# Layer 2's linear attention and graph convolution change places in a four-layer graph transformer kernel

## The reference, cut to what matters

```python
xn = _layernorm(x)
x = x + _L2_gnn_ref(xn, edge_index, W, b) + _L2_mix_ref(xn[None], Wq, bq, Wk, bk, Wv, bv, Wo, bo)[0]
x = x + _L2_ffn_ref(_layernorm(x)[None], ...)[0]

# _L2_gnn_ref: graph convolution, loops added to the edges
norm = deg_inv_sqrt[src] * deg_inv_sqrt[dst]
out = segment_sum((x @ W)[src] * norm[:, None], dst) + b

# _L2_mix_ref: linear attention, 12 heads of 64
q, k, v = elu1(x @ Wq + bq), elu1(x @ Wk + bk), x @ Wv + bv     # elu1(t) = elu(t) + 1
kv, ksum = einsum('bhnd,bhne->bhde', k, v), k.sum(axis=2)
out = (einsum('bhld,bhde->bhle', q, kv) / einsum('bhld,bhd->bhl', q, ksum)) @ Wo + bo
```

## Time and profile before

| what | value |
|---|---|
| median of 3 runs | 3227.3 us (3222.09 to 3234.06) |
| profiled execution, time | 3223.88 us |
| profiled execution, span on the core | 3222.1 us |
| PE busy | 3017.0 us (94%), mean granted clock 0.97 |
| PEld, DVE, ACT, POOL busy | 2340.4, 1723.8, 742.5, 1435.7 us |
| DMA | 256.96 MB, 80 GB/s |

### The profile page before, as it was taken

How to read it: one execution, slowest core, us unless ns; L and a number is a source line. 1 busy time by engine, 2 the same in 40 slices (tenths; PEclk the granted TensorE clock), 3 DMA queues, 4 the chain that set the end, 5 groups by cost and what they waited for, 6 DMA issues and landing times.

```text
span 3222.1 us, 38156 instructions
## 1 busy us (share of the span) xinstructions
PE 3017.0 (94%) x13743; PEld 2340.4 (73%) x13753; DVE 1723.8 (53%) x2816; ACT 742.5 (23%) x1288; POOL 1435.7 (45%) x1007
## 2 busy tenths in 40 slices
PE   8999898999999996998998889899999998999988
PEld 3467576878888884776877358578888886878855
DVE  7734699575545537745785645533333336743132
ACT  1043211242223312102235221211111112212122
POOL 2022377624454442464541044456666664545610
PEclk9999999999999998998999899999999999999999
DMA  2011257311222221222210142123323332222313
GB/s 84 15 44 45 98 178 219 94 39 60 73 69 74 73 65 59 71 89 63 81 53 30 50 132 64 59 76 98 93 88 98 97 98 64 79 68 75 102 36 137
DMA packets 91282, 256.96 MB, mean 80 GB/s; under 512 B 10343, under 2 KB 10983, under 8 KB 90868
## 3 DMA queue, kind: packets, MB, share of 16 engines
q1 hardware_dynamic: 79488, 217.09, 22.1%
q10 hardware_dynamic: 11668, 38.19, 3.5%
HBM read 253.67 MB, written 1.57 MB: 79 GB/s over the span
## 4 chain that ended last, share of the span: by engine, by line
PE 84%; DVE 10%; issue 4%; ACT 2%; DMA 0%; ACTq 0%; DVEq 0%
PE ps L437 23%; PE ps L441 22%; PE ps L442 22%; PE ps L921 3%; DVE aux L2130 2%; PE ps L549 1%; PE ps L543 1%; PE ps L802 1%; PE ps L813 1%; PE ps L795 1%; PE ps L787 1%; DVE hot L2583 1%; DVE row L1938 1%; PE ps L622 1%; PE ps L1008 1%
## 5 line engine op out<-in xcount | busy, mean ns | idle before, releaser
L372 POOL TENSOR_SCALAR w_hi<-raw 128x768 fp32r<-128x768 f32 x498 | 469.3, 942 | 1607.5 <-PE ps L437 1418.3
L375 POOL TENSOR_TENSOR w_lo<-raw,w_hi 128x768 fp32r<-128x768 f32 x498 | 974.9, 1958 | 41.5
L437 PE MATMUL ps<-A_hi,w_hi 128*128 128x512 f32 x924 | 364.5, 394 | 2.2 <-DVE sel_now L2411 1.5
L441 PE MATMUL ps<-A_lo,w_hi 128*128 128x512 f32 x924 | 360.7, 390 | 0.0
L442 PE MATMUL ps<-A_hi,w_lo 128*128 128x512 f32 x924 | 360.2, 390 | 0.0
L437 PE MATMUL ps<-H_hi,w_hi 128*128 128x512 f32 x804 | 319.3, 397 | 22.3 <-issue 11.6
L441 PE MATMUL ps<-H_lo,w_hi 128*128 128x512 f32 x804 | 316.4, 394 | 0.0
L442 PE MATMUL ps<-H_hi,w_lo 128*128 128x512 f32 x804 | 315.9, 393 | 0.0
L437 PE MATMUL ps<-B_hi,w_hi 128*128 128x512 f32 x576 | 234.4, 407 | 13.6 <-DVE B_lo L1916 7.4
L441 PE MATMUL ps<-B_lo,w_hi 128*128 128x512 f32 x576 | 226.6, 393 | 0.0
L442 PE MATMUL ps<-B_hi,w_lo 128*128 128x512 f32 x576 | 226.5, 393 | 0.0
(11 more groups left out here) (510 smaller groups left out, 5632.3 us busy)
## 6 DMA issues: line engine op xcount, KB each, us to landing
raw<-stream_dram SPq DMA_DIRECT2D x552, 384.0 KB, 3.0
w_ring<-w_dram ACTq DMA_DIRECT2D x43, 384.0 KB, 3.8
u_rows<-rows_dram ACTq DMA_DIRECT2D x8, 768.0 KB, 6.0
rows<-rows_dram ACTq DMA_DIRECT2D x7, 768.0 KB, 4.0
w_last<-w_dram ACTq DMA_DIRECT2D x9, 384.0 KB, 3.6
x<-x_dram ACTq DMA_DIRECT2D x1, 1536.0 KB, 8.9
out_dram<-x ACTq DMA_DIRECT2D x1, 1536.0 KB, 5.1
orf<-orf_dram ACTq DMA_DIRECT2D x6, 192.0 KB, 3.1
```

The costliest lines, as they stand in the source:

```text
L372: pool.tensor_scalar(w_hi[:, b // 3, b % 3], raw[:, b // 3, b % 3], 1.0, 1.0, ALU.mult, ALU.mult)\
L375: pool.tensor_tensor(w_lo[:, b // 3, b % 3], raw[:, b // 3, b % 3], w_hi[:, b // 3, b % 3], ALU.subtract)\
L437: mm = pe.matmul(o, wh, xh, start=first, stop=False, skip_group_check=True)
L441: pe.matmul(o, wh, xl, start=False, stop=False, skip_group_check=True)
```

## The change

The attention part of layer 2 goes ahead of the graph convolution: in `TURNS`, on PE, ACT and DVE, and in the weight stream. The loop inside `linear_attention` states that the same banks are pending when it begins and when it ends. So at the end of layer 1's ffn banks 0 and 1 are now given back once more, by two small memsets of DVE behind the last addition into x, and PE notes them as pending; the next norm's first two sums wait for them.

```diff
-TURNS = dict(mix0=3 + 1 + 8, gnn0=16, ffn0=7, mix1=4, gnn1=2, ffn1=4, gnn2=1, mix2=4, ffn2=24, mix3=4, gnn3=1, mlp3=8, ffn3=5)
+TURNS = dict(mix0=3 + 1 + 8, gnn0=16, ffn0=7, mix1=4, gnn1=2, ffn1=4, mix2=4, gnn2=1, ffn2=24, mix3=4, gnn3=1, mlp3=8, ffn3=5)
...
                 done(mm, 6, "dve")
+                S.pending[0] = S.pending[1] = "dve"
 
             if ran("gnn2") or ran("mix2"):
                 norm_of(x)
+            if part("mix2"):
+                turn_t(H, "dve", linear_attention(A, "attention2"))
             if part("gnn2"):
                 turn_n(A, "act", since=normed)
                 graph_t("dve", True)
-            if part("mix2"):
-                turn_t(H, "dve", linear_attention(A, "attention2"))
             if part("ffn2"):
...
             if "gnn2" in parts or "mix2" in parts:
                 norm(x, acc, A)
+            if "mix2" in parts:
+                load_rows(ROW_KV2)
+                linear_attention("attention2", "L2_mix_bq")
             if "gnn2" in parts:
                 spread_high()
                 features_n()
-            if "mix2" in parts:
-                load_rows(ROW_KV2)
-                linear_attention("attention2", "L2_mix_bq")
...
                 freed(dve.tensor_tensor(x[:, :, 0:NCLS], x[:, :, 0:NCLS],
                                         ps[:, 6, 0:48].rearrange("p (f n) -> p f n", n=8)[:, :, 0:NCLS], ALU.add), 6)
+                for b in range(2):
+                    freed(dve.memset(junk[:, 15:16], 0.0), b)
...
             if "gnn2" in parts or "mix2" in parts:
                 norm(x, acc, A, 1e-5)
+            if "mix2" in parts:
+                linear_attention("attention2", 0.0)
+                add_t(x, "L2_mix_bo")
             if "gnn2" in parts:
                 spread_low()
                 features_n(marked=True)
                 add_t(x, "L2_gnn_b")
-            if "mix2" in parts:
-                linear_attention("attention2", 0.0)
-                add_t(x, "L2_mix_bo")
...
-    if "gnn2" in parts:
-        cols_of(v["L2_gnn_W"])
     if "mix2" in parts:
         thirds(v["L2_mix_Wk"], v["L2_mix_Wv"], v["L2_mix_Wq"])
         cols_of(v["L2_mix_Wo"])
+    if "gnn2" in parts:
+        cols_of(v["L2_gnn_W"])
```

## The result

| kernel | median of its runs, us | span of the profiled run, us |
|---|---|---|
| before | 3227.66 (20 runs, 3221.78 to 3234.06) | 3222.1 |
| after | 3233.45 (20 runs, 3227.32 to 3238.71) | 3230.8 |

The ratio of the times is 1.0018, with a 95% interval from 1.0011 to 1.0025. The change makes the kernel 5.8 us slower: inside the half per cent that was called "same", 3 us above the forecast, and clear of zero in so many runs. The page of the profile shows the same work in more time.

The account below looks back on a forecast made before the run. PE, busy 94% of the time, was taken to bound the kernel. First attention group +5.2, features -1.9 and memsets +0.1 summed to +3.4 us, giving a forecast median of 3230.5 us, range 3222 to 3240.

Parts of the forecast that it names:

- the seam that was taken apart: Graph convolution to attention in layer 2: PE has no stall there, so the change has nothing to win.
- Norm to attention: Layer 2's first attention group, fed 3 matmuls a chunk, takes 13.8 us in place of 8.64: +5.2, bounds +3.8 and +9.0.
- Features at full clock: Layer 2's features' product, now behind the projection, starts warm: 25.0 us in place of 26.9, -1.9, bounds 0 and -1.9.
- three q_t waits of 1.5: Inside layer 2's attention loop: PE's three waits for q_t stay at 1.5 us each.
- POOL's cover: Projection to features: POOL needs 8.2 us to split three blocks and has 11.9 us, so no wait; 0.
- The memsets: End of layer 1's ffn: two DVE memsets that the next norm's first sums wait for, +0.1 us, bounds 0 and 0.3.
- The exit keeps its 3.2 us ... 0: Exit of layer 2's attention loop: PE's 3.2 us wait for bank 0 stays, as the same projection follows; 0.
- rival 1: Behind layer 2: clock releases shifted by the change come early at up to five places; 3223.7 us, chance 0.06.
- Late releases that come early: Five places behind layer 2 could each gain 1.1 us from earlier clock release, ending at 3223.7 us; chance 0.06.
- Half pace through the whole first group: Layer 2's first attention group: clock stays low throughout, +9.0 there, +7.2 in all, 3234.5 us; chance 0.08.
- POOL a group behind: Layer 2's features: POOL gets blocks only after the projection, PE waits 8.2 us twice; +24, 3251 us; chance 0.03.
- The order never on the path: Layer 2's two starts, features first or attention first, cost alike: 3227.3 us; chance 0.05.

Follow-up runs that it names:

- a_pairs: Changed kernel, layer 2's first attention group taking two node tiles chunk by chunk, 6 matmuls for each chunk, then the other two: 3226.47 us, ratio 0.9993 against before.
- b_again: The kernel before run once more, unchanged: 3229.77 us, ratio 1.0002 against before.
- a_again: The changed kernel run once more, unchanged: 3233.39 us, ratio 1.0022 against before.
- b_warm: Kernel before with seven warming matmuls on PE ahead of the first chunk of layer 2's norm: 3225.83 us, ratio 0.9992.
- a_warm: Changed kernel with seven warming matmuls on PE ahead of the first chunk of layer 2's norm: 3234.41 us, ratio 1.0023 against before.
- b_sparse: Kernel before with the features' first group going tile by tile, 3 matmuls for each chunk in place of 12: 3229.8 us, ratio 1.0007.
- b_pairs13: Kernel before with pairs of node tiles taken chunk by chunk in the first group of attentions 1 and 3 alone: 3244.53 us, ratio 1.0043.

## Why the prediction was right, by its steps

The mechanism held: no gain at the seam that was taken apart, a dearer start, cheaper features, no block late. That the sum came so close, +3.7 us in layer 2 for +3.4, is in part luck: 0.7 us too much for the first group and 0.4 too much for the end of the layer stand against 1.1 too little at the exit and 0.3 in small parts. And the sum was a sum for layer 2 alone; the runs show some 3 us more outside it, and the median is 5.8 us up where 3.4 were forecast.

**Norm to attention, the main term: right in kind, 0.7 us too dear.** Forecast 13.8 us, measured 13.16. The last chunk's first matmul starts 1903.74 - 1898.21 = 5.5 us after the first, 5.6 forecast. The half pace ended 7.2 us after the start, not 8.6 as in both rows of layers 1 and 3: 1.4 us earlier, and half of that is time. The waits are three of 0.2 us where four of 0.3 were forecast. That this start is what makes the order dear, and not some seam, is shown by a_pairs: with that start alone changed, ratio 0.9993 in place of 1.0018 and 1.0022. Its own share is the smaller one, though. From layer 1's attention to the end the profiled a_pairs is 10.3 us shorter than after: 2.5 in the first group, 2.8 in the projection, 0.4 in the norm and router behind, 1.6 among the experts and 3.1 behind the start of layer 3's attention, all but the first in places that the edit doesn't touch.

**Features at full clock: right.** -1.8 for -1.9, at a clock of 1.00. The rest of attention, the graph product, three q_t waits of 1.5 and the exit of 3.2 us are as forecast.

**POOL's cover: right.** Its first split for the features started at 2020.94 and the features at 2032.82, 11.9 us later, the figure read off layer 3. No wait for w_lo.

**The memsets: twice the price.** +0.2 us in place of +0.1, since PE now waits 0.56 us in front of the norm's first sums and waited 0.35 before; inside the bounds.

**"The exit keeps its 3.2 us ... 0": the wait is as forecast and the term isn't.** It is +1.1 us. Half pace behind the exit lasts from 2005.28 to 2011.29, 6.0 us; in before it began 0.8 us into the projection and lasted 3.4 us, behind an equal pause. The prediction took the wait for the whole of this place's cost. What the runs showed is that the length of half pace behind it belongs to the kernel as it is built and not to the order as such. It came back in the second execution of both kernels, 3.4 us in b_again and 6.0 in a_again; but b_warm, in the old order, has 6.1 us there, and in the new one a_warm has 3.4 and a_pairs none. So it is a release that shifts with what runs ahead of it, as rival 1 had it for the places behind, and it came out against the change; the prediction gave this place no such term.

**Behind layer 2: a term that the prediction did not have.** Of the 8.7 us between the two spans layer 2 explains 3.7. Another 3.2 lie behind the start of layer 3's attention, 1.4 of them in that group (15.47 for 14.09 us). It isn't the order as such: b_warm and b_sparse, in the old order, have 15.36 us for that group and 503.4 us to the end, a_pairs in the new one 14.18 and 501.2. Nor is it chance: b_again has 14.11 and 501.05, a_again 15.46 and 503.55. The last 1.9 us lie ahead of layer 2 in code that the change doesn't touch.

What differs from one execution to the next lies elsewhere. The start of layer 1's attention falls between 1509.9 and 1522.1 us in the twelve profiled kernels that leave everything ahead of it alone, 1512.73 and 1518.82 for the same kernel in before and b_again. From there to the end, two executions of one kernel agree:

| from layer 1's attention to the end | first execution | second |
|---|---|---|
| before | 1709.4 | 1709.4 |
| after | 1716.7 | 1716.1 |

So the change costs 7 us here, a little more than the medians say: 3.7 to 3.8 in layer 2, 2.5 to 3.2 from layer 3's attention on, and 0.4 to 0.5 between layer 1's attention and layer 2. Why these later releases settle at other lengths in another kernel is not shown; that they do is why only 2.7 us, the first group's 4.5 less the features' 1.8, can be called the price of the two starts.

**The rivals.** Late releases that come early: no, together they came late, and rival 1 had the mechanism with the sign reversed. Half pace through the whole first group: no, it ended at 7.2 of 13.2 us. POOL a group behind: no. The order never on the path: no, the interval excludes 1. Not forecast either was how well it could be told: the prediction took 0.5% as the least that a run can tell, and 20 runs told 0.18%.

## What to carry to other kernels

A product right behind a norm that delivers by chunks should have enough work for each chunk to fill the interval between two at PE's low pace; which product that is decided here what an order costs, and reordering its own loops repaired it. A gain at one start is worth what the whole kernel says: in b_warm 1.8 us at the features went again at later places that nobody had touched. An earlier finish on PE also starts whoever waits for its buffers: before an early group is made denser, look at what the engine that gets the blocks will then run beside. And an idle stretch put down to "issue" in front of a matmul deserves a look at the banks in the code: here two such waits, in layers 2 and 3, were worth 6 to 8 us.

## What the runs showed of the hardware

- Full clock won ahead of the first matmul can be lost inside the group: in a_warm PE went from 0.12 to 0.21 us for a 256-column matmul 3.5 us into a group that had waits of 0.5 to 0.6 us between threes of matmuls, and stayed there for 7.1 us, waits or not. Without warming the half pace in that place lasted 7.2 us. Under 12 matmuls of 384 columns for a chunk the same warming kept the full clock through all 25.25 us of the features (b_warm).
- Equal pauses are followed by unequal half pace. Behind 3.2 us at the exit: 3.4, 6.0, 6.1 us and none; behind 7.2 to 7.4 us in front of densely or thinly fed products: 4.0, 3.7, 7.2, 8.6 and, for layer 3 in after, 11.6 us. A second execution of the same kernel gave the same lengths to within 0.4 us: before and b_again 3.97 and 3.66 (features), 3.4 and 3.4 (exit), 8.6 and 8.6 (layer 3); after and a_again 7.2 and 7.2, 6.0 and 6.0, 11.6 and 11.6.
- DVE's product of two tiles in SBUF takes 0.68 us alone and 2.33 us when it starts beside POOL's w_lo split, 3.4 times as long; its subtraction for A_lo takes 0.68 us alone and 1.31 beside the w_hi split (b_pairs13). When POOL's w_hi split started just ahead of the product, in before, the product kept its 0.68 us and the split took 2.27 in place of 0.84.
